# The order of the two score matmuls of a pair in a fused attention and expert kernel

## The reference

```python
x = x + layernorm(attention(layernorm(x), Wq, Wk, Wv, Wo))
x = x + layernorm(experts(layernorm(x), router, gate_up, down))

# attention, for each of 8 batches and 16 heads
score = einsum('bhnd,bhmd->bhnm', q, k) / sqrt(16), masked to m <= n
out = einsum('bhnm,bhmd->bhnd', softmax(score), v)
```

## Time and profile before

| | |
|---|---|
| time, median of 3 runs | 1985.06 us (1983.34 to 1986.63) |
| profiled execution, its own time | 1990.88 us |
| its span | 1989.1 us |
| mean granted TensorE clock | 0.976 |
| busy TensorE / DVE / ACT / GpSimd | 93% / 80% / 66% / 47% |

### The profile page before, as it was taken

The page is one execution under the profiler, slowest core; times in us unless marked ns, Lnnn a source line. Parts: engine busy times, 40 slices in busy tenths (PEclk is TensorE's granted clock), DMA queues, the critical chain, the costliest instruction groups (busy, mean ns, idle before and its releaser), DMA issues.

```text
span 1989.1 us, 76386 instructions
## 1 busy us (share of the span) xinstructions
PE 1856.1 (93%) x26830; PEld 1288.3 (65%) x26831; DVE 1584.2 (80%) x5285; ACT 1320.5 (66%) x3387; POOL 936.8 (47%) x1439
## 2 busy tenths in 40 slices
PE   6799999999999999999999899999999999999980
PEld 3245555555555555555444369899999999999970
DVE  3788888988888888988898648778777777777767
ACT  5177788888888888888777765554445454544436
POOL 4333354456656566566554744444333333333336
PEclk9699999999999999999999999999999999999995
DMA  7733656565655556464557469889899989998848
GB/s 208 211 119 129 194 174 210 166 209 164 192 156 179 176 162 201 143 199 150 159 165 216 139 211 260 236 258 258 257 264 257 266 259 263 262 263 244 242 120 341
DMA packets 257628, 411.79 MB, mean 207 GB/s; under 512 B 36912, under 2 KB 194352, under 8 KB 250160
## 3 DMA queue, kind: packets, MB, share of 16 engines
q1 hardware_dynamic: 217856, 363.46, 57.1%
q0 software_dynamic: 29680, 35.41, 9.9%
q10 hardware_dynamic: 9792, 8.93, 1.5%
HBM read 284.83 MB, written 122.28 MB: 205 GB/s over the span
## 4 chain that ended last, share of the span: by engine, by line
PE 82%; DVE 8%; issue 4%; ACT 2%; DMA 2%; SPq 1%; POOL 1%; DVEq 1%; ACTq 0%; POOLq 0%
PE ps_s L1540 18%; PE ps_s L1372 12%; PE ps_o L1424 11%; PE ps_e L1372 11%; PE ps_w L1372 10%; PE ps_e L1540 6%; PE ps_e L1557 6%; PE ps_o L1557 5%; DVE cmax L797 2%; DVE arena L794 2%; PE ps_e L1550 1%; DVE space L128 1%; ACT space L1272 1%; PE ps_w L1500 1%; ACT arena L1164 1%
## 5 line engine op out<-in xcount | busy, mean ns | idle before, releaser
L1164 ACT ACTIVATE arena<-ps_e 128x512 f32<-128x512 f32 (+3 forms) x1536 | 683.1, 497 | 199.7 <-PE ps_e L1372 195.6
L1372 PE MATMUL ps_e<-arena 98*32 98x512 bf16 (+3 forms) x6144 | 519.1, 329 | 22.4 <-ACT arena L1164 21.9
L1372 PE MATMUL ps_s<-arena 96*32 96x512 bf16 (+3 forms) x6144 | 510.4, 333 | 22.7 <-DVE rmax L794 5.7
L797 DVE TENSOR_REDUCE cmax<-ps_s 128x1 f32<-128x512 f32 x512 | 338.0, 680 | 22.7 <-PE ps_s L1372 21.1
L1372 PEld LDWEIGHTS ps_s<-arena 96*32 96x32 bf16 x6144 | 183.2, 96 | 208.2 <-DVE rmax L794 76.9
L794 DVE CUSTOM_DVE_ANT_0 arena<-ps_s,c,cmax 128x128 bf16<-128x128 f32 (+3 forms) x512 | 269.8, 541 | 47.1 <-PE ps_s L1372 40.3
L1424 PE MATMUL ps_o<-arena 128*32 128x512 f32 (+3 forms) x3072 | 295.4, 487 | 4.7 <-ACT ot L1178 3.0
L794 DVE CUSTOM_DVE_ANT_0 arena<-ps_s,c 128x128 bf16<-128x128 f32 (+3 forms) x512 | 233.4, 482 | 62.7 <-PE ps_s L1372 59.0
L1372 PEld LDWEIGHTS ps_e<-arena 98*32 98x32 bf16 x6144 | 180.0, 97 | 157.8 <-issue 53.2
L669 POOL DMA_INDIRECT acc<-blank,place_now x135 | 212.3, 1573 | 143.3 <-POOL place_now L662 65.7
L1540 PE MATMUL ps_s<-arena 128*128 128x128 f32 x2192 | 268.6, 276 | 1.1 <-ACT arena L1311 0.8
(11 more groups left out here) (182 smaller groups left out, 3034.0 us busy)
## 6 DMA issues: line engine op xcount, KB each, us to landing
arena<-in_gate_up SPq DMA_DIRECT2D x91, 1024.0 KB, 6.2
arena<-qk_parts SPq DMA_DIRECT2D x384, 128.0 KB, 3.0
c_h<-in_gate_up SPq DMA_DIRECT2D x44, 1024.0 KB, 6.0
qk_parts<-space SPq DMA_DIRECT2D x120, 192.0 KB
d_xin<-xs SPq DMA_DIRECT2D x136, 130.5 KB, 3.4
arena<-v_aug SPq DMA_DIRECT2D x32, 512.0 KB, 5.7
o_t<-ot SPq DMA_DIRECT2D x64, 256.0 KB
v_aug<-space SPq DMA_DIRECT2D x28, 512.0 KB, 5.1
```

What stands on the lines that cost most here:

```text
L797: dve.reduce_max(cmax[:, par, i - NB:i - NB + 1], ps_s[:, m % RS, 0:w], AX.X).then_inc(s_cmax, 1)
L1164: act.activation(pw[:, at % RP, begin:end], ps_e[:, n % RE, 0:w], ACT.Exp, scale=SCALE).then_inc(e_done, 1)
L1372: last = pe.matmul(out[at:at + QUAD], lhsT[:, at:at + QUAD], rhs, start=start, stop=stop)
```

## The change

In each pair of each slot the exponential set is now issued first, before the transpose of the maxima and the maximum set. Only TensorE's list changes; nothing is added or removed, and the lists of the other engines stay as they are.

```diff
                 for s in range(4):
                     m = (g - BEGIN) * 4 + s
+                    if 0 <= g + 1 < NE * QUADS:
+                        exp_scores(g + 1, s)
                     if NM <= m < HEADS * NM + NM and m % NM == ROWS_AT:
                         max_rows(m // NM - 1)
                     if 0 <= m < HEADS * NM:
                         max_scores(m)
-                    if 0 <= g + 1 < NE * QUADS:
-                        exp_scores(g + 1, s)
                     if s == 0:
                         for n in groups_due(27, NEVER, g):
                             rank(n)
```

## The result

The changed kernel takes 1997.93 us (median of 4 runs, 1996.9 to 1998.81) beside 1985.85 us of the kernel before on the same chip (4 runs): ratio 1.0058, 95% interval 1.0043 to 1.0073. It is slower by 12 us (8.5 to 14.5). The forecast was 1984.5 us, no change, with a range of 1981 to 1989 us.

The account below looks back on a forecast made before the run. TensorE was taken to set the pace, so only its standstills could be won. Usual quads -0.6, router wait +0.8, early quads -0.2, late quads -0.5 sum to -0.5 us: 1985.06 becomes about 1984.5 us, range 1981 to 1989.

Parts of the forecast that it names:

- Step 1: Place 11.2, 24 quads: +0.16 us there, -0.06 from ACT's chain starting earlier at 10.2; sum +0.10 us a quad.
- Step 2: Place 3.1: the exponential set goes into the wait, -0.22 us, with the DVE ending 0.06 later; sum -0.16 us.
- Step 3: Places 4.2 and 4.3: +0.22 us of lost cover less 0.16 from ACT's earlier feed; +0.06, bounds 0 and +0.22.
- Step 4: Rest of a usual quad, slots 5 to 10: TensorE passes any shift on and DVE slack absorbs later sets; cost 0.
- Step 5: Router wait for a DVE operation behind the maximum of place 6.1, fed later: +0.16 us, five quads, +0.8 us.
- Step 6: Five early quads: -0.11 us at 5.3, +0.10 at 11.2, slots 3 and 4 about even; together -0.2 us.
- Step 7: Five late quads, waiting mostly for the DVE: -0.1 us a quad, bounds +0.1 and -0.4; -0.5 us in all.
- two signs of being wrong: A new repeated wait for the DVE in slots 5 to 10, or quads shrinking by over 0.15 us.
- the DVE as the new wait: DVE fed later at some eight places a quad, half of 0.16 us each reaching TensorE: 16 us slower, 2001; chance 0.16.
- Borders that drain: Borders with other work drain TensorE, 0.15 us at each of 8 products a quad, 30 quads: 36 us, 2021; chance 0.02.
- ACT ahead: ACT, fed 0.06 to 0.22 us earlier 12 times a quad, loses its waits at 4.2 and 4.3: -7 us, 1978; chance 0.2.

Follow-up runs that it names:

- only_112: Kernel before with the exponential set first at slot 11 pair 2 alone; ratio 1.0026 to the kernel before.
- old_in_ten_slots: Changed kernel with the old order in slots 6 to 10 of quads 28 and 29 alone; ratio 1.0013 to the kernel before.
- hybrid: Changed kernel with the old order at places 11.2, 4.2, 4.3 and in slots 6 to 10 of quads 28 and 29; 1980.15 us against 1986.79 before, ratio 0.9970.
- head_only: Kernel before with the exponential set first only in slots 0 to 335 (quads 0 to 27 and lead-in); ratio 1.0033 to the kernel before.
- before_two_swaps: Kernel before with the copy L827 put ahead of L825 in quad 28 and two memsets ahead of L916; ratio 1.0011 to the kernel before.
- before_memsets_4: Kernel before with four memsets of one unused column ahead of L825 in quad 28; ratio 1.0004 to the kernel before.
- moved_two: Changed kernel with L825 and its copy in quad 28, and L916, each one maximum earlier; ratio 1.0056 to the kernel before.
- before_two_waits: Kernel before with L825 of quad 28 one maximum earlier and L916 one maximum later; ratio 1.0012 to the kernel before.
- tail_only: Kernel before with the exponential set first only in quads 28 and 29; ratio 1.0033 to the kernel before.
- before_again: The kernel before, unchanged, run and traced once more on another chip; ratio 1.0006 to the kernel before.

## Why the prediction was wrong

Its steps 1 to 3 held. Step 1: the waits around 11.2 went from 0.93 + 0.08 + 0.07 to 1.18 us, +0.10 as worked out, though by another way: +0.25 at the place itself, less the two small waits ahead of it, which the text had not named. That the size came out is in part luck: made alone, in only_112, the same exchange cost 0.17 us a quad. Step 2: 0.34 to 0.18, -0.16. Step 3: 0.24 to 0.30, +0.06.

Step 4 put the rest of a quad at 0 and the sum was taken as -0.03; the quad grew by 0.07. Steps 1 to 3 make 0.00 of that as measured; 0.05 lie around the small matmul group behind place 6.2 (`ps_w<-w_r,h_t`). Step 5 had +0.16 for the router wait; it went from 0.54 to 0.78, and its four quads grew by 0.31. Quads 5 to 24 were to cost 0.2 us by these steps and cost 2.0. Step 6 had -0.2 for the early quads; they cost 0.1. That is most of the 2.3 us that the trace shows up to quad 28, near the 2.6 us (0.8 to 4.6) of old_in_ten_slots. That much is a size slightly off, and near what a measurement can tell.

Step 7 failed. It had -0.5 us for the five late quads. Quad 25 cost 0.2, quads 26 and 27 gave 0, and quads 28 and 29 cost 5.5 us. The failure stands in the sentence behind that step, that "the loads and GpSimd's work wait for the same signals" and so shift along. They shift against the DVE: GpSimd's run hangs on the exponentials, and the DVE's list on the maxima. In quad 29 the DVE's L916 started 0.11 us ahead of L686 before, and 0.27 us behind it now, a shift of 0.38 us; in quad 28 L825 started 0.38 us behind L686 before and 0.41 now, a shift of 0.03. A sign of the first was in the trace of before, in a row that the prediction did not read: the L686 that took 1.06 us instead of 0.64. A contest decided by 0.11 us, beside a change that feeds the two sides at other times by up to 0.22 us each, was the rival that was missing. How near the second one stood to turning, no row of the trace of before tells.

Neither of the prediction's own two signs of being wrong came: the quads did not shrink, and no new repeated wait for the DVE stands in slots 5 to 10. The kernel was slower by two single waits, for which it had no sign.

The rival "the DVE as the new wait" had the right side and the right engine, but its mechanism, half of 0.16 us at eight places, did not occur: no new repeated wait stands in slots 5 to 10 on this chip. "Borders that drain" fell: the sets at the borders with other work still follow in 0.22, 0.16, 0.11 and 0.06 us. "ACT ahead" is what the hybrid reached in part, by leaving out the places where the new order costs.

**What stays open.** First, the timed difference is 12.1 us (8.5 to 14.5) and the positions give 8.6 up to the last exponential set; the 2.7 us behind it may be chance. Second, on the chips where before took 2002 to 2006 us the head alone cost 6.6 us, three times as much. There TensorE has a wait of its own at 7.3 in most quads from 10 on: 0.21 to 0.29 us in the old order, 0.43 to 0.51 in the new; and the copy L827 met GpSimd's run three times in head_only (1.25 us instead of 0.2, in quads 16, 20 and 24). That these two make up the rest was not tried. Third, what exactly lets a DVE instruction through between two of GpSimd's. Fourth, a wait for a whole run was never brought about in the old order, so its price there is not known.

## What to carry to other kernels

A change of order is worth its standstills place by place, and each place can be priced from start-to-start distances; take the order at each place by whether the wait there is for the set that now goes first. The hybrid was built so, and is the one kernel here that gained 0.3%. Before calling a shift free, look for pairs of DVE and GpSimd instructions that overlap and read SBUF, above all for one whose time is longer than its group's mean: it shows a contest that a small shift can turn (0.38 us did for L916, 0.03 us for L825), at the price of GpSimd's whole run. A tuned order can depend on such a chance. The small instruction can be moved clear of the run, but time it afterwards: of the moves tried here one landed in the run again and one made a new wait.

## What the hardware showed beside this

A DVE instruction that came second mostly waited not for one GpSimd instruction but for all that followed without a gap: L825 took 2.29 us through four of them and 2.89 us through the end of L745 and four, and L916 2.32 us through three, where they take 0.20 and 0.68 us undisturbed. The exception is before_two_swaps, where L916 waited for one. At nearly the same distance the outcome differs: 0.38 to 0.41 us after L686, L825 got through at L686's end in the old order, at 0.41 in the changed kernel it did not, and at 0.42 in before_memsets_4 it did; at 0.59 it got through at once. And 0.2 us ahead of L686, beside L745, it waited for the whole run in moved_two and for nothing in before_two_waits.

On some chips the exponential of place 7.0 starts late, and I found nothing in the trace to account for it: in tail_only the set of 868.05 (quad 22) was taken up at 868.89, in the kernel before the set of 863.00 at 863.50, with the same sets around both. In before_again the quads from 10 to 23 are 0.9 to 1.4 us longer than in the first profile, except for the three with a router wait (0.1 us or less): together 11 of the 14 us by which its span is longer. ACT's timeline of tail_only:

```profile
868.89 1.09 ACT L1164 ACTIVATE arena<-ps_e 128x512 f32<-128x512 f32 x2 [0.76 <-PE ps_e L1372]
```
